# Attention block with a gated FFN on one core: silus alternate with casts, VectorE's low halves stand a chunk later, other GpSimd shares, a third statistics buffer

## What is computed

```python
x = x + attn(layernorm(x))     # scores = (xn @ W_qk) @ xn.T * 128**-0.5 + (kpos - qpos) * slope, causal
                               # softmax(scores) @ (xn @ W_v.T)
x = x + ffn(layernorm(x))      # h = silu(xn @ wg.T) * (xn @ wu.T);  h @ wd.T
                               # wg, wu: 384 x 128, wd: 128 x 384, integers times 1/127
```

## Time and profile before

| | us |
|---|---|
| median of three runs | 143.6 |
| lowest, highest | 143.3, 144.7 |
| the profiled execution, its own time | 143.12 |
| its span in the trace | 141.1 |
| DVE busy (share of the span) | 119.3 (85%) |
| PE busy | 119.1 (84%) |
| ACT busy | 109.4 (78%) |
| POOL busy | 103.4 (73%) |

### The profile page before, as it was taken

One profiled execution on the slowest core, in us unless ns is written; L12 is line 12 of the kernel. 1 busy time (PEld: TensorE's weight loads), 2 busy tenths in 40 slices (PEclk: granted clock), 3 DMA queues, 4 the chain that ended last, 5 costly groups with the idle time before them and its releaser, 6 DMA issues.

```text
span 141.1 us, 3405 instructions
## 1 busy us (share of the span) xinstructions
PE 119.1 (84%) x1183; PEld 88.1 (62%) x1183; DVE 119.3 (85%) x336; ACT 109.4 (78%) x249; POOL 103.4 (73%) x162
## 2 busy tenths in 40 slices
PE   0278578999999999889999998988994789979961
PEld 0066164768987869777869975667842545656661
DVE  0759989998788995989987969998869999998892
ACT  4035779999966999757999949977869689988920
POOL 6491789964992545996895999479669999995810
PEclk9999999999999999999999999999999999999999
DMA  4896000000000000000000001643001303057625
GB/s 133 230 255 177 3 2 2 5 2 0 5 0 0 5 0 2 0 5 0 0 5 0 5 0 40 99 89 79 0 5 37 79 0 79 6 73 213 198 78 153
DMA packets 18515, 7.28 MB, mean 52 GB/s; under 512 B 9152, under 2 KB 18496, under 8 KB 18496
## 3 DMA queue, kind: packets, MB, share of 16 engines
q1 hardware_dynamic: 18496, 7.02, 20.6%
HBM read 2.82 MB, written 2.10 MB: 35 GB/s over the span
## 4 chain that ended last, share of the span: by engine, by line
PE 32%; DVE 27%; POOL 14%; ACT 13%; DMA 5%; issue 5%; SPq 2%; DVEq 0%; POOLq 0%
DVE probsT_lo L805 5%; POOL hidden_lo L411 5%; PE work_ps L553 5%; PE attn_ps L566 3%; DVE biased L822 3%; DVE stats L707 3%; PE score_ps L501 3%; PE score_ps L503 3%; DMA x2T_lo<-xn_lo 3%; PE attn_ps L568 3%; PE attn_ps L567 3%; PE score_ps L502 3%; ACT probs L960 3%; ACT probsT_hi L982 2%; DVE xs L832 2%
## 5 line engine op out<-in xcount | busy, mean ns | idle before, releaser
L566 PE MATMUL attn_ps<-v_hi,probsT_hi 128*128 128x128 f16 x144 | 25.8, 219 | 2.4 <-DVE xs L832 1.7
L805 DVE TENSOR_TENSOR probsT_lo<-work_ps,probsT_hi 128x512 f16<-128x512 f32 (+3 forms) x48 | 25.2, 553 | 3.0 <-ACT probsT_hi L982 2.7
L960 ACT ACTIVATE probs<-biased,neg_max 128x128 f32<-128x128 f32 (+7 forms) x32 | 25.0, 783 | 3.2 <-DVE neg_max L822 3.1
L982 ACT CAST probsT_hi<-work_ps 128x512 f16<-128x512 f32 (+3 forms) x48 | 21.4, 483 | 6.4 <-PE work_ps L553 6.2
L822 DVE CUSTOM_DVE_ANT_0 biased<-score_ps,bias,neg_score_scale 128x128 f32<-128x128 f32 (+7 forms) x32 | 25.8, 806 | 0.6 <-PE score_ps L503 0.6
L568 PE MATMUL attn_ps<-v_hi,probsT_lo 128*128 128x128 f16 x144 | 25.8, 219 | 0.0
L567 PE MATMUL attn_ps<-v_lo,probsT_hi 128*128 128x128 f16 x144 | 25.7, 219 | 0.0
L553 PE MATMUL work_ps<-ident,probs 128*128 128x128 f32 x144 | 21.4, 274 | 1.3 <-DVE probsT_lo L805 0.7
L707 DVE BATCH_NORM_STATS2 stats<-xs 128x6 f32<-128x128 f32 x64 | 15.2, 283 | 5.2 <-DMA xs<-in_L_attn_x_dram 3.7
L553 PEld LDWEIGHTS work_ps<-ident,probs 128*128 128x128 f32 x144 | 16.5, 141 | 4.4 <-DVE probsT_lo L805 1.0
L566 PEld LDWEIGHTS attn_ps<-v_hi,probsT_hi 128*128 128x128 f16 x144 | 14.1, 98 | 5.5 <-DVE probsT_lo L805 1.8
(11 more groups left out here) (138 smaller groups left out, 331.5 us busy)
## 6 DMA issues: line engine op xcount, KB each, us to landing
out_dram<-xs SPq DMA_DIRECT2D x7, 256.0 KB, 3.2
xs<-in_L_attn_x_dram SPq DMA_DIRECT2D x3, 512.0 KB, 8.2
xs<-in_L_attn_x_dram SPq DMA_DIRECT2D x2, 256.0 KB, 3.1
out_dram<-xs SPq DMA_DIRECT2D x2, 128.0 KB, 2.0
wgu_int<-in_L_ffn_w_gate_dram SPq DMA_DIRECT2D x1, 192.0 KB, 3.0
wgu_int<-in_L_ffn_w_up_dram SPq DMA_DIRECT2D x1, 192.0 KB, 3.1
wd_int<-in_L_ffn_w_down_dram SPq DMA_DIRECT2D x1, 192.0 KB, 3.5
x2T_hi<-xn_hi SPq DMA_TRANSPOSE x8, 2.5
```

What stands on the lines that cost most here:

```text
L566: pe.matmul(attn_ps[:, 0:D], p_hi, v_j, start=(j == 0), stop=False)
L805: dve.tensor_tensor(probsT_lo[:, i % 2, cols], work_ps[:, bank, 0:n], probsT_hi[:, i % 2, cols], ALU.subtract).then_inc(work_emptied, 1)
L960: act.activation(probs[:, i % 2, 0:n], biased[:, i % 2, 0:n], ACT.Exp, bias=neg_max[:, i:i + 1], scale=-1.0, accum_out=prob_sum[:, i:i + 1 ...
L982: act.copy(probsT_hi[:, i % 2, CW * h:CW * h + n], work_ps[:, bank, 0:n]).then_inc(probsT_hi_ready, 1)
```

## The change

Four edits, in the FFN but for the last:

1. ACT: the silus of chunk 0 stand alone; then silu (c+1, j) and cast (c, j) alternate for j = 0 to 2, and a token_high that was due at c stands behind them. The casts of chunk 7 stand at the end, without silus between.
2. DVE: the low halves of chunk c - 1 follow the multiplies of chunk c and add_ffn(c - 2); those of chunk 7 stand at the end.
3. POOL takes 0, 1, 2, 2, 2, 3, 3, 1 blocks, so all three of chunks 5 and 6.
4. Norm 4 gets a statistics buffer of its own, and its first bn_stats waits for nothing. Norm 5 waits until POOL has read norm 3.

```diff
-        stats = sb("stats", [P, 2, TB, 6], F32)
+        stats = sb("stats", [P, 3, TB, 6], F32)
...
+        def stats_of(n):
+            return 2 if n == B else apart(n)
...
         def pool_blocks(c):
-            return 0 if c == 0 else 1 if c in (1, NCH - 1) else HB - 1
+            return (0, 1, 2, 2, 2, 3, 3, 1)[c]
...
             def statistics(n, j):
-                if j == 0 and n not in (0, 1, B + 3):
-                    dve.wait_ge(pool_step, steps_before(n) - N_STEPS + N_READ)
+                if j == 0 and n not in (0, 1, B, B + 3):
+                    dve.wait_ge(pool_step, steps_before(n - 1 if n == B + 1 else n) - N_STEPS + N_READ)
...
                 if c >= LAG:
                     add_ffn(c - LAG)
-                hidden_low(c)
+                if c:
+                    hidden_low(c - 1)
+            hidden_low(NCH - 1)
             add_ffn(NCH - 2)
...
+            silus(0, 0)
             for c in range(NCH - 1):
-                silus(c, c % 2)
+                for j in range(HB):
+                    silus(c + 1, (c + 1) % 2, [j])
+                    hidden_high(c, [j])
                 for n, h in {0: [(B + 2, 0)], 1: [(B + 2, 1)], 3: [(B + 3, 0)], 4: [(B + 3, 1)]}.get(c, []):
                     token_high(n, h)
-                hidden_high(c)
-            silus(NCH - 1, (NCH - 1) % 2, range(HB - 1))
-            hidden_high(NCH - 1, range(1))
-            silus(NCH - 1, (NCH - 1) % 2, range(HB - 1, HB))
-            hidden_high(NCH - 1, range(1, HB))
+            hidden_high(NCH - 1)
```

More of the change, by code:

```diff
@@ L349, in moments @@
             def moments(n):
-                steps, stat = steps_before(n), stats[:, apart(n), :, :]
+                steps, stat = steps_before(n), stats[:, stats_of(n), :, :]
                 half, quarter, per_element, eps, power = (norm_const[:, k:k + 1].broadcast_to([P, TB]) for k in range(5))
@@ L701, in statistics @@
             def statistics(n, j):
-                if j == 0 and n not in (0, 1, B + 3):
-                    dve.wait_ge(pool_step, steps_before(n) - N_STEPS + N_READ)
+                if j == 0 and n not in (0, 1, B, B + 3):
+                    dve.wait_ge(pool_step, steps_before(n - 1 if n == B + 1 else n) - N_STEPS + N_READ)
                 if j == 0 and B <= n < B + 3:
                     dve.wait_ge(attn_added, TB * (n - B + 1))
-                m = dve.bn_stats(stats[:, apart(n), j, :], at(xs, TB * (n % B) + j, slice(0, D)))
+                m = dve.bn_stats(stats[:, stats_of(n), j, :], at(xs, TB * (n % B) + j, slice(0, D)))
                 if j == TB - 1:
```

## The result

The changed kernel takes 148.0 us, the median of four runs (147.06 to 148.17); the kernel before takes 143.5 beside it. The ratio is 1.028, with a 95% interval of 1.022 to 1.034: slower, as forecast, but by 4.5 us where 2.2 were forecast, and outside the range of 143.2 to 147.0. The profiled execution took 148.14, with a span of 146.1.

What follows compares the result with a forecast made beforehand. No engine was taken as the bound by itself; what waits for what sets the end. Third buffer -0.7, late chunk 6 +1.5 and the end +1.4 gave +2.2, so 143.6 + 2.2 = 145.8 us, range 143.2 to 147.0.

Steps and rivals of the forecast that it cites:

- Third buffer: Attention of batch 1: of DVE's 1.51 us wait for POOL, 0.68 is gained, since ACT's cast is late next; -0.7.
- Start of the FFN: Chunk 0's low halves take 3.8 us beside POOL's passes; down(0) starts at 111.7, gate_up(3) at 113.1, 0.2 earlier.
- Chunks 3 to 5: Chunk 1's low halves are ready at 116.8, PE waits 1.1 for down(1), gate_up(4) starts at 118.2; +1.0, hidden in +1.5.
- The xn_hi cast of norm 7: Cast behind chunk 4's silus, its transpose lands later, gate_up(6) starts at 127.7 against 126.23; +1.5 (+0.7 to +2.3).
- The end: From gate_up(7) to the last addition, 9.5 us against 8.1, through POOL's three blocks and port waits; +1.4.
- The sum: Whole kernel: -0.7 + 1.5 + 1.4 = +2.2 us.
- the port costs nothing: Rival: low halves of chunks 0 and 1 take 0.60 each, gate_up(6) starts 2.6 earlier; 141.7 us, chance 0.12.
- 1.2 beside the step: Start of the FFN: without the low halves' waits for xn_lo and centring the sum would be 1.2 lower.
- A quick landing and a short end: Rival: gate_up(6) at 126.9 (+0.7), the end costs 0.6; +0.6 in all, 144.2 us, chance 0.26.

Runs made afterwards that it cites:

- POOL's short passes: Changed kernel with five POOL passes (xn_lo (6, 0), centrings and scalings of norm 7) cut to 8 of 128 columns; 145.44 us, ratio 1.013.
- the 20 transposes: Changed kernel with 20 transposes of the identity on PE ahead of down(0), into a PSUM bank nobody reads; 145.76 us, ratio 1.014.
- the pair of medians 145.69 and 144.67: The run with xn first, 145.69 us, and the same with 20 transposes of the identity on PE ahead of down(0), 144.67 us.
- xn first: Changed kernel with ACT's token_high ahead of the three silu-cast pairs and POOL's xn_lo of norm 7 ahead of its low halves; 145.69 us, ratio 1.015.
- the old shares: Changed kernel with the old GpSimd shares (two blocks of chunks 5 and 6); 148.26 us, ratio 1.034.
- the new shares on the old order: Kernel before with third buffer, POOL's xn_lo of norm 7 ahead of its low halves of chunks 3 and 4, and the change's shares; 141.92 us, ratio 0.988.
- the better version: Kernel before with third buffer and POOL's xn_lo of norm 7 ahead of its low halves of chunks 3 and 4; 141.89 us, ratio 0.987.
- the run with the silus alone: Kernel before with only ACT's new order, silus of the next chunk alternating with casts of this one; single execution, 157.22 us.

## Why the prediction was right in sign and wrong in size

- *Third buffer, -0.7.* Right to a hundredth: the pair is 1.90 apart and waits 0.84 for ACT's cast, so the pair is 0.67 closer. Alone -0.8.
- *Start of the FFN, -0.2 and no more.* The low halves were right: 3.69 for three, forecast 3.8; down(0) at 111.72, forecast 111.7. The run with POOL's short passes showed the cause. That DVE's two-input instruction and POOL's exclude each other, as the Trainium skill, page "SBUF — State Buffer", section "Who interferes with whom", says, agrees with that run (1.98 for 3.69). But the next step, "ends at 113.1, where gate_up(3) begins", failed: it took down(0) at the length of the earlier trace rows. That sum leaves PE idle until 111.7, 2.57 us in the trace, and the prediction never asks what else this does: it put the clock at nothing. The clock halved, and gate_up(3) began at 114.25. This cost 1.1 by the 20 transposes (gate_up(4), 119.28 to 118.21) and 1.0 by the pair of medians 145.69 and 144.67.
- *Chunks 3 to 5, +1.0 by down(1).* Gate_up(4) came at 119.28, which less 0.11 is 119.2, against the forecast of 118.2; the whole difference is the clock. PE's wait ahead of down(1) was 0.47 and not 1.1, since the slow matmuls had filled the rest.
- *The xn_hi cast of norm 7, +1.5.* The mechanism was right and was, with its slow landing, the largest single loss (2.3 by the run with xn first). Cast at 123.61, forecast 122.55, late by the clock's 1.0; xn_lo and POOL as forecast. The landing was the second term mis-sized: 4.31, where I took the middle of 2.4 and 4.04. "(+0.7 to +2.3)" held its upper end; with both terms at their measured size the step is +3.5.
- *The end, +1.4.* 9.53 against the forecast of 9.5. That its cost was "inside" the shares was wrong, though: the old shares leave 9.7, the new shares on the old order 8.1. It is the two edits of order, about 0.7 by the low halves alone and the rest, by difference, with the alternation.
- *The sum.* +2.2, plus 1.0 for the clock, plus 1.1 for the landing, is 4.3; the medians are 4.5 apart. The rival "the port costs nothing" was refuted by the 3.69, and its mirror, POOL's passes cut short, gained 2.6, about 1.0 of it the clock. The prediction had two prices for these waits, 1.2 beside the step and 4.1 by this rival's 141.7, and the run gives neither. "A quick landing and a short end" failed at both.

The range was too narrow for a plain reason: it had bounds for the terms that I had listed, and the clock was not listed, although the forecast itself held an idle PE of 2.6 us where PE's waits of before, in the FFN, were at most 1.9.

## What to carry to other kernels

When an edit moves PE's idle time from two waits into one, add up the new wait and read the granted clock of the slice behind it; here one gap of 2.6 us cost another 1.1, while gaps of 1.9 and 1.3 before the change, and the one of 2.24 ahead of gate_up(6) after it, cost nothing more. A cheap subtraction on VectorE is cheap only where GpSimd has no full pass over 512 columns beside it, so choose its place by what GpSimd does there. And ahead of reordering three engines, look at who is at the head of the chain of the wait: moving two GpSimd instructions, each past two others, gave 1.0 us (142.90 to 141.89), while the new order of two engines cost 5.

## What the runs showed of the hardware

**The clock falls behind some waits of PE and not behind others of the same length.** In three of the four executions of the changed kernel the mean granted clock was 0.988 (147.87 to 148.17 us), in the fourth 1.0 (147.06), 0.8 to 1.1 us apart. From 95 us on in the profiled executions, the clock fell behind idle times of PE of 2.57 us (twice) and 3.2 to 3.3 (three times), but also behind one of 1.97 (POOL's short passes) and one of 2.22 (the better version). It stayed full behind waits of 2.07, 2.12, 2.24, 2.38 and 2.75. So it is partly a matter of chance here, and a part of the spread of such a kernel. The Trainium skill, page "TensorE: Matmul & The Clock Gate", Part 1, says that the clock has these two rates and follows how busy the array has lately been; the windows above agree.

**Who is kept back depends on POOL's instruction.** POOL's rstd, on 128 x 8 elements, took 1.63 to 1.66 us wherever it ran in the thirteen profiles, with one exception: in the four kernels that have the three low halves of chunk 0 beside the rstd of norm 7, that one took 2.03 or 2.04. There POOL lost 0.4 us, and the three low halves took 1.90. Beside passes over 512 columns DVE lost (3.69 us for three). Why the two differ is not shown.

**The DMA transposes that land late all have an instruction packet near their issue.** The changed kernel's transfer of 125.51 and the late one of the earlier trace rows landed in 4.3 and 4.0 where 2.5 is usual:

```profile
x2T_lo<-xn_lo SPq DMA_TRANSPOSE x1, 4.3
```

The DMA queues of 127.5 to 128.0 us show, 2.1 us behind its issue and 2.2 ahead of its landing, one packet of another queue:

```profile
q8 instruction: 1, 0.02, 13.4%
```

In the thirteen profiles 104 transposes were issued from 100 us on. 30 landed in 2.8 to 4.4 us, and all 30 have such a packet between half a microsecond ahead of their issue and 2.6 behind it; of the 74 that landed in 2.4 to 2.6, nine do. By and large a later packet goes with a later landing: 2.8 for three at 0.4, 3.3 for one at 0.8 (the xn_hi transpose of 123.38 before), 3.8 for one at 1.0, 4.3 for the one at 2.1. But four with a packet 0.3 to 0.4 ahead of their issue took 3.2 to 3.3, and seven with one at 2.2 to 2.4 behind it landed in 2.4 to 2.5 all the same. Two transposes issued one behind the other are not by themselves late (2.4 and 2.5 in the run with the silus alone). This was only read from the profiles: no run moved a packet and nothing else, so that it causes the delay isn't shown. It would explain why a landing can change by 1.9 us with an edit that doesn't touch it, and it was the part of the forecast for which I had taken a middle value.
